# Last layer of a four-layer network: TensorE takes the attention sums two groups back and between a group's two pairs of turned scores

## The chip, the cores and the metric

The kernel runs on one core of one Trainium2 chip. The metric is the device time of one execution in microseconds (us). The time before is 2976.93 us, the median of three runs that lay between 2975.23 and 2987.77.

## The reference

The network has four layers over x, float32 of shape (4, 1024, 128). Each layer normalizes x without weights and adds an attention-like block and a feed-forward block. Only the last layer matters here:

```python
qkv = (x @ W_qkv + b_qkv).reshape(b, s, h, 3 * hd)        # h = 16 heads of hd = 8
logits = jnp.einsum('bshd,bkhd->bhsk', q, k) / np.sqrt(hd)
logits = jnp.where(k_pos > q_pos, -jnp.inf, logits)       # s = 1024
attn = jax.nn.softmax(logits, axis=-1)
out = jnp.einsum('bhsk,bkhd->bshd', attn, v).reshape(b, s, d)
attention = out @ W_out + b_out
# experts: the two best of 8 for each token, C = 128, H = 512
h = new_gelu(x_flat @ w1[e].T + b1[e]); out_e = h @ w2[e].T + b2[e]
output = output + cw[:, e:e + 1] * out_e
```

## The kernel before

The stage in question is `attn3_stage`. It computes the last layer's attention and its experts together, as one sequence of **slots** written out by hand. An item is one batch with one set of four heads; there are 16 items (4 batches, 4 sets). In slot s TensorE does three things with three different items.

- **Plain scores** of item s (`score`, L2138): queries on the partitions, keys along the row. VectorE takes the largest of each row from them (`largest`, L2354). There are 20 such units in an item; `SHARE` spreads them over the slot as 2, 2, 1, 1, 2, 2, 2, 2, 2, 2, 1, 1. A unit on the diagonal adds its mask by four more short matmuls (L2154). Here the units are called S.
- At the slot's start it turns the maxima of item s - 1 (`turn_max`, L2159), once VectorE has reduced the last unit of the slot before and put the maxima together (L2452). GpSimd splits them into bfloat16 parts, and they go by DMA into extra rows beside the queries.
- **Turned scores** of item s - 2 (`scoreT`, L2164): keys on the partitions, queries along the row, the maxima subtracted by the extra rows. ScalarE takes the exponential (`exps`, L2301). GpSimd zeroes the triangle of a diagonal tile (`causal`, L2487). Then TensorE multiplies by the values (`sums`, L2181), four float32 matmuls, one for each head, side by side in one bank.

A slot has 12 **groups**, one for each pair of a 512-query half and a 128-key tile: groups 0 to 3 belong to the first half, 4 to 11 to the second. Groups 0 to 3 and 8 to 11 lie on the diagonal and are 512, 384, 256 and 128 queries wide; the others are 512 wide. A group wider than 256 has four turned units and is issued as two pairs, here T0 and T2; a narrower one has two units and one pair, T0 alone. The order in a group is T0, S, T2, S, then the sums of the group before, then extras.

The **extras** are: XT (turn the rows of an expert tile, L2203, groups 0 to 3), UP (first expert matmul, L2211, a burst at group 4; ScalarE's gelu, L2321, follows each), DOWN (second expert matmul, L2222, from group 7), X (turn the finished sums, `turn_sums` L2196; half 1 of the item before in group 2, half 0 in group 6), A and Y (turn the merged heads and project them out, L2232 and L2244, in every fourth slot, groups 4 and 5, then 8 and 9). There are 39 expert tiles over slots 2 to 13, three or four in a slot. In slots 14 to 17 GpSimd gathers the experts' outputs, two indirect DMAs behind each of its triangles (L2491, L2496). Slots 16 and 17 have no S.

Three resources set when TensorE may go on.

- The **score ring**: two pairs of PSUM banks. S, the turned maxima, XT, DOWN, X, A and Y all take the next pair in turn, and each waits until the one two places before it has been read by VectorE:

```python
def take_s(*key):
    n = s_at[key]
    if n >= 2:
        pe.wait_ge(s_read, n - 1)
    return sbank(n)
```

- The **turned ring**: three banks for T and UP. A pair waits until the unit two before its first has been read by ScalarE (L2171). T2 thus waits for the first exponential of T0, and the next T0 for the first exponential of T2.
- One bank for the sums. ScalarE copies it out after each half (`out`, L2294: half 1 after the exponentials of the next item's group 0, half 0 after those of group 4, ahead of the gelus), and the first sums of the next half wait for that copy (L2185).

Of the kernel before, what the change touches and what calls it, by code (L numbers as in the profile page):

```python
# [1674 lines left out]
NI = B * NG  # L1675
# [224 lines left out]
GROUPS = len(TILES)  # L1900
SHARE = (2, 2, 1, 1, 2, 2, 2, 2, 2, 2, 1, 1)
BURST = 4
FIRST_SLOT, LAST_SLOT = 2, 13
PER_SLOT = {s: range((s - FIRST_SLOT) * NTILE // (LAST_SLOT + 1 - FIRST_SLOT),
                     (s + 1 - FIRST_SLOT) * NTILE // (LAST_SLOT + 1 - FIRST_SLOT))
# [22 lines left out]
TU = [list(turned_units(g)) for g in range(GROUPS)]  # L1928
# [7 lines left out]
def merged_batch(s):  # L1936


    return (s - 6) // 4 if s >= 6 and (s - 6) % 4 == 0 else None


def ring_tables():

    s_at, t_at = {}, {}

    def add(table, key):  # L1950
        table[key] = len(table)

    for s in range(SLOTS + 1):
        b = s - 2
        back = 0 <= b < NI
        if 0 <= s - 1 < NI:
            add(s_at, ("Z", s - 1))
        for g in range(GROUPS):
            if back:
                for i in range(len(TU[g])):  # L1960
                    add(t_at, ("E", b, g, i))
            for i in range(sum(SHARE[:g]), sum(SHARE[:g + 1])) if s < NI else ():
                add(s_at, ("S", s, i))
            for j, kt in enumerate(tiles_of(s)):
                if g == j:
                    add(s_at, ("XT", kt))
                if g == BURST:
                    for x in range(2):
                        add(t_at, ("UP", kt, x))
                if g == 7 + j:  # L1970
                    add(s_at, ("DOWN", kt))
            if g == 2 and b >= 1:
                add(s_at, ("X", b - 1, 1))
            if g == 6 and back:
                add(s_at, ("X", b, 0))
            if merged_batch(s) is not None and g in (4, 5):
                add(s_at, ("A", merged_batch(s), g - 4))
            if merged_batch(s) is not None and g in (8, 9):
                add(s_at, ("Y", merged_batch(s), g - 8))
    return s_at, t_at  # L1980


def attn3_stage(k, R):
# [15 lines left out]
    with ExitStack() as ctx:  # L1999
# [19 lines left out]
        s_at, t_at = ring_tables()  # L2019
# [25 lines left out]
        with nc.Block() as block:  # L2045
# [81 lines left out]
            def _(pe):  # L2127
# [128 lines left out]
                for s in range(SLOTS + 1):  # L2256
                    f, b = s, s - 2
                    front, back = f < NI, 0 <= b < NI
                    bb = merged_batch(s)
                    if 0 <= s - 1 < NI:  # L2260
                        turn_max(s - 1)
                    for g in range(GROUPS):
                        units = range(sum(SHARE[:g]), sum(SHARE[:g + 1])) if front else ()
                        for i in range(0, len(TU[g]), 2):
                            if back:
                                scoreT(b, g, i)
                            if front and i // 2 < len(units):
                                score(f, units[i // 2])
                        for i in units[len(TU[g]) // 2:]:
                            score(f, i)  # L2270
                        if back and g > 0:
                            sums(b, g - 1)
                        if g == 0 and 0 <= b - 1:
                            sums(b - 1, GROUPS - 1)
                        for j, kt in enumerate(tiles_of(s)):
                            if g == j:
                                turn_rows(kt)
                            if g == BURST:
                                for x in range(2):
                                    up(kt, x)  # L2280
                            if g == 7 + j:
                                down(kt)
                        if g == 2 and 0 <= b - 1:
                            turn_sums(b - 1, 1)
                        if g == 6 and back:
                            turn_sums(b, 0)
                        if bb is not None and g in (4, 5):
                            turn_out(bb, g - 4)
                        if bb is not None and g in (8, 9):
                            out_project(bb, g - 8)  # L2290

            @block.scalar
            def _(act):
                def out(c, half):  # L2294

                    act.wait_ge(sums_done, c * GROUPS + (4, GROUPS)[half])
                    if c > 0:
                        act.wait_ge(s_done, s_at["X", c - 1, half] + 1)
                    act.copy(oT[:, half, :], k.ps[:, bankO, :]).then_inc(sums_copied, 1)  # L2299

                def exps(c, g):  # L2301
                    w = WIDTH[g]
                    for i, (r, es) in enumerate(TU[g]):
                        n = t_at["E", c, g, i]
                        act.wait_ge(t_done, n + 1)
                        if i == 0 and c * GROUPS + g >= 3:
                            act.wait_ge(sums_done, c * GROUPS + g - 2)
                        hd = 2 * r + es[0]
                        dst = pT[:, g % 3, hd:hd + len(es), 0:w]
                        src = k.ps[:, tbank(n), 0:len(es) * w].rearrange("p (h q) -> p h q", q=w)  # L2310
                        act.activation(dst, src, ACT.Exp).then_inc(t_read, 1)  # L2311

                def gelu(kt, x):

                    n = t_at["UP", kt, x]
                    act.wait_ge(t_done, n + 1)
                    if kt >= 4:
                        act.wait_ge(s_done, s_at["DOWN", kt - 4] + 1)
                    for f in range(HALF_F):
                        ff = x * HALF_F + f  # L2320
                        a = act.activation(h[:, kt % 4, ff, :], k.ps[:, tbank(n), f * NSLOT:(f + 1) * NSLOT],  # L2321
                                           ACT.Gelu_apprx_tanh, bias=b1[:, kt % 4, ff:ff + 1])
                    a.then_inc(t_read, 1)

                for s in range(2, SLOTS + 1):
                    c = s - 2
                    for g in range(GROUPS):
                        if c < NI:
                            exps(c, g)
                        if g == 0 and c > 0:  # L2330
                            out(c - 1, 1)
                        if g == 4 and c < NI:
                            out(c, 0)
                        if g == BURST:
                            for kt in tiles_of(s):
                                act.wait_ge(s_t[kt % 4], 16 * 4 * (kt // 4 + 1))
                                for x in range(2):
                                    gelu(kt, x)

            @block.vector  # L2340
            def _(dve):
# [85 lines left out]
                for s in range(SLOTS + 1):  # L2427
                    f, b = s, s - 2
                    bb = merged_batch(s)
                    if 0 <= s - 1 < NI:  # L2430
                        turned_max(s - 1)
                    for g in range(GROUPS):
                        for i in range(sum(SHARE[:g]), sum(SHARE[:g + 1])) if f < NI else ():
                            largest(f, i)
                        for j, kt in enumerate(tiles_of(s)):
                            if g == j:
                                rows_turned(kt)
                            if g == 7 + j:
                                down_done(kt)
                        if g == 2 and 0 <= b - 1:  # L2440
                            norm(b - 1, 1)
                        if g == 6 and 0 <= b < NI:
                            norm(b, 0)
                        if bb is not None and g in (4, 5):
                            out_turned(bb, g - 4)
                        if bb is not None and g in (8, 9):
                            residual(bb, g - 8)
                    if f < NI:
                        dve.wait_ge(s_read, s_at["S", f, len(SU) - 1] + 1)
                        if f >= 2:  # L2450
                            dve.wait_ge(s_done, s_at["Z", f - 2] + 1)
                        dve.tensor_reduce(m[:, f % 2, :], mx[:, f % 2].rearrange("p r e t x -> p (r e t) x"), AX_X, ALU.max)\  # L2452
                           .then_inc(max_done, 1)
                    if s - 1 in GATHER:
                        combine(GATHER[s - 1])
# [215 lines left out]
```

## Time and profile before

| | |
|---|---|
| median of 3 runs | 2976.93 us (2975.23 to 2987.77) |
| profiled execution | 2986.29 us, span 2984.6 us |
| TensorE busy | 2085.2 us, 70% of the span |
| VectorE, ScalarE, GpSimd busy | 64%, 48%, 45% |
| this stage, slots 2 to 17 | from about 2236 to 2956 us of the span |

A timeline row has a start, a length, engine, line, operation, output and inputs, the partitions and elements, and how many instructions the row joins. In brackets stands the recorded idle time before it and the instruction that ended it. Matmuls are pipelined: a row's length includes the way through the array, so the time that a step takes of TensorE is read from start to start. A float32 matmul shows as two records. The line numbers are those of the kernel before; in the changed kernel every line behind the new constant stands one or a few lower.

### The profile page before, as it was taken

Reading aid. Unit: us, or ns where it says so; the run is one execution under the profiler, and the core shown is the slowest. Engines: PE = TensorE matmul, PEld = TensorE weight load, DVE = VectorE, ACT = ScalarE, POOL = GpSimd, SP = SyncE. Lnnn points to the kernel's source line nnn. Section 1 sums busy time; section 2 is a strip of 40 time slices with the busy share of each in tenths; the row PEclk is TensorE's granted clock in tenths of the full one; section 3 lists DMA queues with packets and bytes.
Section 4 is the critical chain, followed back from the end, with each engine's and each line's share of the span. In section 5 each row is a group of like instructions: output and inputs, shape, how many; then the busy total and the mean of one; then the engine's idle time right before and its main releaser. Section 6 shows DMA issues by size and latency. Waiting matters only on the chain. (4 is left out here: it accounts for less than half of the span.)

```text
span 2984.6 us, 35273 instructions
## 1 busy us (share of the span) xinstructions
PE 2085.2 (70%) x10366; PEld 1067.6 (36%) x10366; DVE 1922.1 (64%) x2484; ACT 1445.0 (48%) x2523; POOL 1328.7 (45%) x974
## 2 busy tenths in 40 slices
PE   2677786868777666856562688865048888888875
PEld 1233232323323223424341466653014444444422
DVE  6379888888988896683336677773155555656551
ACT  1476665666666652713341433332206656655553
POOL 2277777777777784022002566633521101111253
PEclk9899998989889898878766798876559999999875
DMA  1333434444444442001200000002321322313111
GB/s 39 88 129 126 133 125 128 134 127 136 127 123 133 122 142 73 0 1 50 84 20 0 1 0 0 0 0 50 98 81 46 87 75 65 90 51 87 28 29 49
DMA packets 146984, 214.72 MB, mean 72 GB/s; under 512 B 30746, under 2 KB 58292, under 8 KB 146228
## 3 DMA queue, kind: packets, MB, share of 16 engines
q1 hardware_dynamic: 142756, 204.72, 22.7%
q0 software_dynamic: 4096, 8.40, 1.3%
q8 instruction: 64, 1.05, 0.1%
q14 instruction: 68, 0.56, 0.1%
HBM read 193.91 MB, written 23.86 MB: 73 GB/s over the span
## 5 line engine op out<-in xcount | busy, mean ns | idle before, releaser
L505 PE MATMUL ps<-m_hC,ident 128*128 128x512 f32 x1024 | 547.4, 669 | 241.4 <-DVE m_hC L777 129.5
L694 POOL TENSOR_TENSOR m_dBx<-m_du,m_rowB 128x1024 f32<-128x1024 f32 x256 | 602.7, 2385 | 20.9 <-DVE m_h L768 20.9
L2311 ACT ACTIVATE a_pT<-ps 128x512 f32<-128x512 f32 (+2 forms) x640 | 319.7, 553 | 392.8 <-PE ps L2176 390.9
L2361 DVE TENSOR_REDUCE a_mx<-ps 128x2 f32<-128x1024 f32 (+2 forms) x320 | 349.1, 1116 | 165.1 <-PE ps L2154 126.3
L623 ACT ACTIVATE ps<-m_delta,m_A 128x512 f32<-128x512 f32 x512 | 341.6, 685 | 159.4 <-DVE m_h L768 158.4
L505 PEld LDWEIGHTS ps<-m_hC,ident 128*128 128x128 f32 x1024 | 198.8, 207 | 561.1 <-DVE m_hC L777 213.8
L768 DVE TENSOR_TENSOR_SCAN m_h<-ps,m_carry,m_dBx 128x512 f32<-128x512 f32 x256 | 311.4, 1265 | 74.4 <-ACT ps L623 53.7
L768 DVE TENSOR_TENSOR_SCAN m_h<-ps,m_dBx 128x512 f32<-128x512 f32 x256 | 295.9, 1206 | 63.2 <-ACT ps L623 34.8
L2491 POOL TENSOR_SCALAR_AFFINE_SELECT a_pT<-a_pT 128x512 f32<-128x512 f32 x128 | 81.6, 637 | 517.0 <-ACT a_pT L2311 516.4
L704 POOL TENSOR_TENSOR m_hC<-m_h,m_rowC 128x1024 f32<-128x1024 f32 x64 | 155.9, 2436 | 226.2 <-DVE m_h L768 226.2
L777 DVE TENSOR_TENSOR m_hC<-m_h,ps 128x1024 f32<-128x1024 f32 x192 | 234.2, 1220 | 15.2 <-issue 1.3
L2149 PE MATMUL ps<-a_k,a_q 48*128 48x512 bf16 (+3 forms) x768 | 139.4, 365 | 110.1 <-DMA a_k<-qk_parts 93.8
L633 ACT COPY ps<-m_rowC 128x512 f32<-128x512 f32 x192 | 112.1, 584 | 187.0 <-DVE m_hC L777 186.3
L2191 PE MATMUL ps<-a_pT,l_v 128*9 128x512 f32 (+3 forms) x1536 | 185.9, 560 | 21.7 <-POOL a_pT L2491 21.4
L2176 PE MATMUL ps<-a_q,a_k 51*128 51x512 bf16 (+3 forms) x768 | 129.9, 363 | 70.0 <-ACT a_pT L2311 68.5
L1611 PE MATMUL ps<-c_triu_adt,ones 128*128 128x512 f32 x64 | 53.6, 933 | 93.5 <-ACT c_triu_adt L1582 93.5
L460 PE MATMUL ps<-pad,m_wk 128*128 128x512 f32 x256 | 117.5, 604 | 1.1 <-DVE m_diag L726 1.1
L2176 PEld LDWEIGHTS ps<-a_q,a_k 51*128 51x128 bf16 x768 | 32.5, 95 | 190.6 <-ACT a_pT L2311 156.3
L266 PE MATMUL ps<-ident,n_xn 128*128 128x128 f32 x128 | 35.4, 431 | 84.9 <-DVE n_xn L246 84.8
L1889 POOL DMA_INDIRECT expert_rows<-l_xn,l_slot x64 | 65.3, 1020 | 63.1 <-DVE p_cmp L1855 43.9
L2149 PEld LDWEIGHTS ps<-a_k,a_q 48*128 48x128 bf16 x768 | 40.0, 99 | 129.9 <-issue 94.3
L2228 PEld LDWEIGHTS ps<-a_w,a_h 128*128 128x128 f32 x624 | 73.8, 194 | 34.4 <-DVE a_mx L2361 22.2
(361 smaller groups left out, 3872.2 us busy)
## 6 DMA issues: line engine op xcount, KB each, us to landing
m_rowB<-bc_rows SPq DMA_DIRECT2D x256, 256.0 KB, 3.8
m_rowC<-bc_rows SPq DMA_DIRECT2D x256, 256.0 KB, 3.7
a_w<-in_L3f_w1T SPq DMA_DIRECT2D x39, 256.0 KB, 2.5
a_w<-in_L3f_w2T SPq DMA_DIRECT2D x39, 256.0 KB, 3.2
qk_parts<-p_part SPq DMA_DIRECT2D x24, 256.0 KB
expert_rows<-in_zero_rows SPq DMA_DIRECT2D x39, 128.0 KB, 2.6
a_xs<-expert_rows SPq DMA_DIRECT2D x39, 128.0 KB, 2.2
expert_out<-a_y SPq DMA_DIRECT2D x39, 128.0 KB, 3.1
```

Of the source, the lines that this page charges most:

```text
L460: mm = pe.matmul(o, wk[:, d, tap, c * P:c * P + P], pad[:, b * ROW + shift:b * ROW + shift + CH], start=tap == 0, stop=tap == CONV - 1)
L505: mm = pe.matmul(ps[:, bankY + c, :], k.ident[:], hC[:, n % 3, c, :], start=False, stop=n % NS == NS - 1)
L623: act.activation(ps[:, bankA + m % 3, :], delta[:, i % 2, c, chunk(i, x)], ACT.Exp, scale=An[:, ITEMS[i][0], c, s:s + 1]).then_inc(decayed, 1)
L694: pool.tensor_tensor(dBx[:, n % 3], du[:, i % 2, :, chunk(i, x)], rowB[:, n % 4, :].unsqueeze(1).to_broadcast([P, HALF, CH]), ALU.mult).th ...
L704: pool.tensor_tensor(hC[:, n % 3], h[:, n % 3], rowC[:, n % 4, :].unsqueeze(1).to_broadcast([P, HALF, CH]), ALU.mult).then_inc(hc_pool, 1)
L768: dve.tensor_tensor_scan(time(h[:, n % 3, c, :]), time(ps[:, bankA + m % 3, :]), time(dBx[:, n % 3, c, :]), first, ALU.mult, ALU.add).then ...
L777: dve.tensor_tensor(hC[:, n % 3], h[:, n % 3], ps[:, bankC, :].unsqueeze(1).to_broadcast([P, HALF, CH]), ALU.mult).then_inc(hc_dve, 1)
L2149: mm = pe.matmul(k.ps[:, bank + r, j * w:j * w + w], qs[u][rows, e, t * P:t * P + P], ks[u][rows, e, x:x + w], start=True, stop=not diag, ...
L2176: mm = pe.matmul(k.ps[:, tbank(n + r), j * w:j * w + w], ks[u][rows, e, kt * P:kt * P + P], qs[u][rows, e, q0:q0 + w], start=True, stop=Tr ...
L2191: mm = pe.matmul(k.ps[32 * hd:32 * hd + HD + 1, bankO, CH - w:CH], R["v"][:, c, kt, hd, :], pT[:, g % 3, hd, 0:w], start=kt == 0, stop=kt ...
L2311: act.activation(dst, src, ACT.Exp).then_inc(t_read, 1)
L2361: dve.tensor_reduce(mx[:, c % 2, :, es[0]:es[0] + len(es), t, x // CH], src, AX_X, ALU.max)\
```

## The change

It adds a lag of two groups for the sums and puts them between T0 and T2. Both S units of a four-unit group then follow T2 back to back (`SHARE` has no 3, so the branch that would put one ahead of T2 is never taken). X moves from groups 2 and 6 to 4 and 8, A from 4 and 5 to 6 and 7, Y from 8 and 9 to 9 and 10. ScalarE copies the sums out one group later, which for half 0 is behind the gelus and no longer ahead of them.

```diff
+LAG = 2
...
                     for g in range(GROUPS):
-                        units = range(sum(SHARE[:g]), sum(SHARE[:g + 1])) if front else ()
-                        for i in range(0, len(TU[g]), 2):
-                            if back:
-                                scoreT(b, g, i)
-                            if front and i // 2 < len(units):
-                                score(f, units[i // 2])
-                        for i in units[len(TU[g]) // 2:]:
+                        units = list(range(sum(SHARE[:g]), sum(SHARE[:g + 1]))) if front else []
+                        if back:
+                            scoreT(b, g, 0)
+                        if back and g >= LAG:
+                            sums(b, g - LAG)
+                        if g < LAG and 0 <= b - 1:
+                            sums(b - 1, GROUPS - LAG + g)
+                        if back and len(TU[g]) > 2:
+                            if len(units) > 2:
+                                score(f, units.pop(0))
+                            scoreT(b, g, 2)
+                        for i in units:
                             score(f, i)
-                        if back and g > 0:
-                            sums(b, g - 1)
-                        if g == 0 and 0 <= b - 1:
-                            sums(b - 1, GROUPS - 1)
...
-                        if g == 2 and 0 <= b - 1:
+                        if g == 4 and 0 <= b - 1:
                             turn_sums(b - 1, 1)
-                        if g == 6 and back:
+                        if g == 8 and back:
                             turn_sums(b, 0)
-                        if bb is not None and g in (4, 5):
-                            turn_out(bb, g - 4)
-                        if bb is not None and g in (8, 9):
-                            out_project(bb, g - 8)
+                        if bb is not None and g in (6, 7):
+                            turn_out(bb, g - 6)
+                        if bb is not None and g in (9, 10):
+                            out_project(bb, g - 9)
...
                             exps(c, g)
-                        if g == 0 and c > 0:
+                        if g == LAG - 1 and c > 0:
                             out(c - 1, 1)
-                        if g == 4 and c < NI:
+                        if g == LAG + 3 and c < NI:
                             out(c, 0)
```

VectorE's order and the ring's table follow the same moves.

The first place is TensorE in group 7 of a slot with expert tiles. L2176 is T, L2149 S, L2191 the sums, L2228 DOWN. Before, the group and the T0 of the next:

```order
 L2176 MATMUL ps<-a_q,a_k 128x512 x2
 L2149 MATMUL ps<-a_k,a_q 128x512 x2
 L2176 MATMUL ps<-a_q,a_k 128x512 x2
 L2149 MATMUL ps<-a_k,a_q 128x512 x2
 L2191 MATMUL ps<-a_pT,l_v 9x512 x4
 L2228 MATMUL ps<-a_w,a_h 128x128 x8
 L2176 MATMUL ps<-a_q,a_k 128x512 x2
```

and now (lines one lower):

```order
 L2177 MATMUL ps<-a_q,a_k 128x512 x2
 L2192 MATMUL ps<-a_pT,l_v 9x512 x4
 L2177 MATMUL ps<-a_q,a_k 128x512 x2
 L2150 MATMUL ps<-a_k,a_q 128x512 x4
 L2229 MATMUL ps<-a_w,a_h 128x128 x8
 L2177 MATMUL ps<-a_q,a_k 128x512 x2
```

The sums have gone in front of T2, and DOWN now stands directly behind two S units.

The second place is TensorE in groups 10 and 11, at the end of a slot; L2154 is the mask of an S unit and L2162 turns the maxima. Before:

```order
 L2176 MATMUL ps<-a_q,a_k 128x256 x4
 L2149 MATMUL ps<-a_k,a_q 128x512 x2
 L2154 MATMUL ps<-a_consts_bf 128x128 x4
 L2191 MATMUL ps<-a_pT,l_v 9x384 x4
 L2176 MATMUL ps<-a_q,a_k 128x128 x4
 L2149 MATMUL ps<-a_k,a_q 128x512 x2
 L2154 MATMUL ps<-a_consts_bf 128x128 x4
 L2191 MATMUL ps<-a_pT,l_v 9x256 x4
 L2162 MATMUL ps<-ident,a_m 32x128
```

and now:

```order
 L2177 MATMUL ps<-a_q,a_k 128x256 x4
 L2192 MATMUL ps<-a_pT,l_v 9x512 x4
 L2150 MATMUL ps<-a_k,a_q 128x512 x2
 L2155 MATMUL ps<-a_consts_bf 128x128 x4
 L2177 MATMUL ps<-a_q,a_k 128x128 x4
 L2192 MATMUL ps<-a_pT,l_v 9x384 x4
 L2150 MATMUL ps<-a_k,a_q 128x512 x2
 L2155 MATMUL ps<-a_consts_bf 128x128 x4
 L2163 MATMUL ps<-ident,a_m 32x128
```

No sums stand any more between the slot's last S unit and the turning of the maxima.

The third place is ScalarE from group 4 on, in a slot with three tiles (L2311 exponentials, L2299 the copy of the sums, L2321 gelus). Before:

```order
 L2311 ACTIVATE a_pT<-ps 128x512 x4
 L2299 COPY a_oT<-ps 128x512
 L2321 ACT_TABLE_LOAD
 L2321 ACTIVATE a_h<-ps,a_b 128x256 x12
 L2311 ACT_TABLE_LOAD
 L2311 ACTIVATE a_pT<-ps 128x512 x16
```

and now:

```order
 L2313 ACTIVATE a_pT<-ps 128x512 x4
 L2323 ACT_TABLE_LOAD
 L2323 ACTIVATE a_h<-ps,a_b 128x256 x12
 L2313 ACT_TABLE_LOAD
 L2313 ACTIVATE a_pT<-ps 128x512 x4
 L2301 COPY a_oT<-ps 128x512
 L2313 ACTIVATE a_pT<-ps 128x512 x12
```

The copy has moved from ahead of the gelus to behind the exponentials of group 5.

## Rows read from the trace of the kernel before

**Rows 1.** Busy time by stretch (length, then engines in us, count; PEclk), the stage
```profile
2240.00:2860.00 620.00, 532.08 (x4704) 269.44 (x4703) 355.10 (x443) 370.52 (x743) 112.89 (x197) 0.94 0.23 65
2860.00:2984.60 124.60, 80.81 (x491) 23.82 (x487) 37.23 (x95) 52.17 (x105) 52.55 (x65) 0.64 0.14 39
```

**Rows 2.** The same view, slots 7 and 12, three tiles each
```profile
2473.46:2516.04 42.58, 35.83 (x343) 18.48 (x344) 25.76 (x32) 28.00 (x56) 6.76 (x13) 1.00 0.24 64
...
2703.61:2748.95 45.34, 38.79 (x344) 19.12 (x344) 25.76 (x32) 28.01 (x56) 6.75 (x13) 0.92 0.25 72
```

**Rows 3.** Waits, 2260 to 2860 us: total, times, longest
```profile
ACT a_pT L2311 <- PE ps L2176: 240.7, 143, 7.6
...
PE ps L2176 <- ACT a_pT L2311: 52.9, 92, 2.0
```

**Rows 4.** Timeline of TensorE, group 7 of slot 8 (start, length)
```profile
2542.57 0.39 PE L2176 MATMUL ps<-a_q,a_k 51*128 51x512 bf16 x2
2542.80 0.38 PE L2149 MATMUL ps<-a_k,a_q 48*128 48x512 bf16 x2
2543.64 0.39 PE L2176 MATMUL ps<-a_q,a_k 51*128 51x512 bf16 x2 [0.47 <-ACT a_pT L2311]
2543.87 0.38 PE L2149 MATMUL ps<-a_k,a_q 48*128 48x512 bf16 x2
2544.18 1.05 PE L2191 MATMUL ps<-a_pT,l_v 128*9 128x512 f32 x8
2545.16 2.05 PE L2228 MATMUL ps<-a_w,a_h 128*128 128x128 f32 x16
```

**Rows 5.** Timeline of ScalarE and VectorE in the same group
```profile
2542.99 2.16 ACT L2311 ACTIVATE a_pT<-ps 128x512 f32<-128x512 f32 x4 [1.27 <-PE ps L2176]
...
2543.22 2.36 DVE L2361 TENSOR_REDUCE a_mx<-ps 128x2 f32<-128x1024 f32 x2
```

**Rows 6.** Timeline of TensorE, the end of slot 8
```profile
2557.68 0.38 PE L2149 MATMUL ps<-a_k,a_q 48*128 48x512 bf16 x2
...
2558.40 0.62 PE L2191 MATMUL ps<-a_pT,l_v 128*9 128x256 f32 x8 [0.23 <-POOL a_pT L2491]
2559.84 0.27 PE L2162 MATMUL ps<-ident,a_m 128*32 128x128 f32 x1 [0.82 <-DVE a_m L2452]
```

**Rows 7.** Timeline of ScalarE and TensorE around the burst, slot 8
```profile
2527.86 0.59 ACT L2299 COPY a_oT<-ps 128x512 f32<-128x512 f32 x1
...
2529.84 4.63 ACT L2321 ACTIVATE a_h<-ps,a_b 128x256 f32<-128x256 f32 x12
...
2536.43 0.39 PE L2176 MATMUL ps<-a_q,a_k 51*128 51x512 bf16 x2 [1.99 <-ACT a_pT L2311]
...
2536.97 1.81 PE L2191 MATMUL ps<-a_pT,l_v 128*9 128x512 f32 x8
```

**Rows 8.** Timeline of TensorE and VectorE, groups 0 and 1 of slot 8
```profile
2516.47 0.22 PE L2149 MATMUL ps<-a_k,a_q 48*128 48x128 bf16 x2
...
2517.55 0.28 PE L2149 MATMUL ps<-a_k,a_q 48*128 48x256 bf16 x2
...
2518.09 0.41 PE L2191 MATMUL ps<-a_pT,l_v 128*9 128x128 f32 x8
...
2519.49 0.34 PE L2149 MATMUL ps<-a_k,a_q 48*128 48x384 bf16 x2 [0.35 <-DVE a_mx L2361]
...
2517.09 0.69 DVE L2361 TENSOR_REDUCE a_mx<-ps 128x4 f32<-128x512 f32 x1 [0.46 <-PE ps L2154]
2518.20 1.23 DVE L2361 TENSOR_REDUCE a_mx<-ps 128x4 f32<-128x1024 f32 x1 [0.42 <-PE ps L2154]
```

**Rows 9.** Timeline of GpSimd and TensorE, slots 15 and 16
```profile
2868.65 0.64 POOL L2491 TENSOR_SCALAR_AFFINE_SELECT a_pT<-a_pT 128x512 f32<-128x512 f32 x1 [9.48 <-ACT a_pT L2311]
...
2875.36 1.04 PE L2191 MATMUL ps<-a_pT,l_v 128*9 128x256 f32 x8 [1.63 <-POOL a_pT L2491]
...
2892.03 0.64 POOL L2491 TENSOR_SCALAR_AFFINE_SELECT a_pT<-a_pT 128x512 f32<-128x512 f32 x1
```

More of the change, by code:

```diff
@@ L1971, in ring_tables @@
                     add(s_at, ("DOWN", kt))
-            if g == 2 and b >= 1:
+            if g == 4 and b >= 1:
                 add(s_at, ("X", b - 1, 1))
-            if g == 6 and back:
+            if g == 8 and back:
                 add(s_at, ("X", b, 0))
[L1976 to L1979, printed above, removed]
+            if merged_batch(s) is not None and g in (6, 7):
+                add(s_at, ("A", merged_batch(s), g - 6))
+            if merged_batch(s) is not None and g in (9, 10):
+                add(s_at, ("Y", merged_batch(s), g - 9))
     return s_at, t_at
@@ L2282, in _ @@
                                 down(kt)
-                        if g == 2 and 0 <= b - 1:
+                        if g == 4 and 0 <= b - 1:
                             turn_sums(b - 1, 1)
-                        if g == 6 and back:
+                        if g == 8 and back:
                             turn_sums(b, 0)
-                        if bb is not None and g in (4, 5):
-                            turn_out(bb, g - 4)
-                        if bb is not None and g in (8, 9):
-                            out_project(bb, g - 8)
+                        if bb is not None and g in (6, 7):
+                            turn_out(bb, g - 6)
+                        if bb is not None and g in (9, 10):
+                            out_project(bb, g - 9)
             @block.scalar
@@ L2439, in _ @@
                                 down_done(kt)
-                        if g == 2 and 0 <= b - 1:
+                        if g == 4 and 0 <= b - 1:
                             norm(b - 1, 1)
-                        if g == 6 and 0 <= b < NI:
+                        if g == 8 and 0 <= b < NI:
                             norm(b, 0)
[L2444 to L2447, printed above, removed]
+                        if bb is not None and g in (6, 7):
+                            out_turned(bb, g - 6)
+                        if bb is not None and g in (9, 10):
+                            residual(bb, g - 9)
                     if f < NI:
```

## The prediction

> **What bounds the kernel now.** I read the busy time by stretch first, then the waits, then single groups on the timelines. Only the last layer's attention stage changes. In its long part TensorE is busy 532 of 620 us at a clock of 0.94 of full; its rest has a clock of 0.64 [rows 1]. A slot with three expert tiles that kept the full clock took 42.58 us with TensorE busy 35.83 [rows 2], so 6.75 us of the slot are recorded idle. Read from start to start, where the way through the array isn't counted as work, the waits come to about 8 us a slot. TensorE sets the pace by its work plus its waits, and ScalarE mostly waits for it: 240.7 us against 52.9 the other way [rows 3]. The reader is to see that the wait which the change attacks is real. In group 7 T0 starts at 2542.57 and T2 at 2543.64, 1.07 later, with 0.23 for T0 and 0.31 for one S unit between (2542.57 to 2542.80; 2543.87 to 2544.18) [rows 4]; 0.53 is left idle. That time is the exponential's: ScalarE starts 0.42 after T0 and takes 0.54 for one of its four [rows 5].
>
> **What the change removes.** TensorE's instructions stay the same, so a slot changes by its waits alone. The sums of a 512-wide group take 0.98 (2544.18 to 2545.16) [rows 4]. T0 and sums make 1.21, more than 1.07, so T2 no longer waits where such sums stand before it. Six groups of a slot (0, 4, 6, 7, 8, 9) wait so now, about 0.5 each: 3.0. Narrow sums remain in front of T2 in groups 0, 1 and 4 (256, 128 and 256 wide; scaled from 0.98 to about 0.5, 0.25 and 0.5), and these still wait about 1.1 together. Also removed are the waits for GpSimd's triangle (0.23 to 0.29 in group 11 [rows 6]) and VectorE waits of 0.8 in groups 1 and 2 (one is 0.35 [rows 8]). The copy of half 0 leaves the way of the gelus, 0.59 [rows 7], and X of half 1 moves into the time in which TensorE waits for the burst (the 1.99 behind the gelus [rows 7]); burst waits fall from 3.3 to 2.5. Removed: 3.0 - 1.1 + 0.3 + 0.8 + 0.8 = 3.8 us a slot.
>
> **What it adds.** (a) *The score ring.* VectorE needs 2.36 for two 1024-wide units [rows 5], and TensorE may be two ring places ahead and no more. Before, the two S units of a group stood 1.07 apart with the sums behind them, and what came next found the older unit read. Now S, S and the extra come within 0.6 us, and the extra waits for the first S of its own group. A unit's read starts 0.42 after an unmasked S (as ScalarE's after T0) and 0.62 after a masked one (2516.47 to 2517.09); TensorE goes on 0.06 after the read's end (2518.20 + 1.23 to 2519.49) [rows 8]. Count from T2. Group 9: S at 0.17, read from 0.59 to 1.80, DOWN at 1.86, TensorE free at 0.79: 1.07 of wait. Group 8 (768-wide unit, about 0.95): 0.8. Group 7: group 6 left two units, read until 3.1 after its T2; the next T2 comes 1.07 + 1.21 = 2.28 after it, so the first S of group 7 is read from 3.1 to 4.3, its second S waits 0.3 and DOWN 0.9. Group 0: S at 0.23, read from 0.85 to 1.54, XT at 1.60; the masked units take 0.37 and 0.54 (2517.55 to 2518.09 [rows 8]), TensorE is free at 1.14: 0.46. Group 1 likewise 0.8 behind VectorE's backlog, group 3 0.2. Sum 4.5. (b) *The slot's end.* From the last S to the turned maxima 2.16 pass (2557.68 to 2559.84 [rows 6]): VectorE's last read and the joining of the maxima. Before, sums lay in it, now nothing does; the recorded 0.82, 0.9 from start to start, becomes 2.16 - 0.43 = 1.75: 0.85 more. (c) *The copy.* Sums 4 stand behind T0 of group 6 and need the copy, which ScalarE makes behind the exponentials of group 5. From T2 of group 5 these end at 0.42 + 2 x 0.54, with one more in front, at 1.5; the copy ends at 2.15; T0 is out at 1.3: 0.85 of wait, and 0.2 before T0. The twin in group 2 is covered by XT's wait. Sum 1.05.
>
> Added: 4.5 + 0.85 + 1.05 = 6.4, net **+2.6 us in each of 12 tile slots**, +31. Slots 6 and 10 turn out a batch: A was partly in the burst's wait and now stands visible behind S, S: +1.6 each, +3; slot 14 the same without tiles, +1. Slots 15 to 17 gain. There GpSimd sets the pace: 2868.65 to 2892.03 for eight triangles with two gathers behind each, and TensorE waits up to 1.63 for one [rows 9]. From the last of these to the next slot's first, T2 of group 5 is no longer queued behind a fresh T0 (1.3) and X is out of the way (0.6, at the half clock 1.1), against the copy's 0.85: about -2, -1.5, -1.5, together -5. At an equal clock the sum is +30.
>
> **Clock.** TensorE falls to the lower level (1.2 GHz) in most slots, usually behind the burst: sums take 1.81 behind the 1.99 wait [rows 7] where they take 1.05 at 2.4 GHz [rows 4]. Slot 12 with 0.92 of the clock took 45.34, slot 7 with all of it 42.58 [rows 2]: such a stretch costs up to 2.8. Waits per slot rise from about 8.3 to 10.9, and the 1.75 at the slot's end stands close to those of group 0. I take two or three such stretches more than now, +6 in all, between none and one in each tile slot, 12 x 2.8 = 34. Sum: +36, of 2986.3 for the profiled execution 3022. That execution lay 9.4 above the median, so I forecast 2976.93 + 36 = **3013**.
>
> **Rivals.** *Clock* (slower still): every tile slot gets a second low stretch, 30 + 34 = +64: 3041. The waits at the slot's end speak for it; against it, slot 7 had 6.75 us of idle time and never fell. The Trainium skill (TensorE: Matmul & The Clock Gate, "A second HAM failure mode: psum-queue depth-cycling") tells of a kernel in which small idle stretches between PSUM banks make the clock swing to and fro. By that rule this rival would be the case; the trace before shows falls, but mostly behind long waits.
>
> *The ring doesn't bite* (faster): if VectorE has read the first S by the time TensorE reaches DOWN or XT, the 4.5 is gone, and of the rest +2.6 - 4.5 = -1.9 a slot remains, -23; with the tail's -5 and the +2 that is left of A's 4 it is -26: 2951. The place is DOWN in groups 7 to 9; it decides from a read that ends within 0.8 of T2, against 1.8 worked out above. For it speaks only that VectorE is idle 40% of the stage (355 of 620 busy [rows 1]); against it that the ring is two deep and the third item always needs the first.
>
> *No difference*: ring waits half as long, because an earlier wait in the same group moves T2 later and with it VectorE's backlog shrinks: 36 - 27 = +9, 2986.
>
> That the order isn't what the change says can be excluded: the rows of the order show the sums in front of T2 and both S units behind it.
>
> **Numbers.** A difference of 0.5% (14.9 us) is about what a measurement of this kernel can tell from none. Chances: forecast (2992 to 3030) 0.55, clock 0.15, no difference 0.16, ring doesn't bite 0.14. So slower 0.70, same 0.16, faster 0.14. The range leaves out most of the faster case and the far end of the clock's: 2965 to 3042.
>
> **What would show it.** TensorE's wait before T2 (52.9 now) should fall to under a half outside the burst; new waits of TensorE for VectorE's reads in front of DOWN of about 0.8 to 1.1 and of XT of 0.5 to 0.8; 1.7 instead of 0.82 before the turned maxima; about 0.85 for the copy before sums 4; three-tile slots at full clock of about 45 us; slots 15 to 17 shorter. If DOWN starts without a wait behind S, S, or if a full-clock slot is under 42.6, the prediction is wrong. A GpSimd wait in the tail that doesn't shrink would make only the -5 wrong.

## The result and the profile after

Before took 2984.34 us (median of six runs, 2975.23 to 2995.36), the changed kernel 3036.45 (six runs, 3028.38 to 3042.59). The ratio is **1.0174** with a 95% interval of 1.0145 to 1.0204: slower by 1.7%, or 52.1 us, where 36 us or 1.2% were forecast. The forecast of 3013 was worked out from a median before of 2976.93, of three runs; with six it is 7.4 higher. The profiled execution of the change took 3028.38 us, the lowest of its six.

First the busy time by stretch of the changed kernel. Columns: stretch, length, then busy us (count) of PE, PEld, DVE, ACT, POOL, the granted clock, DMA share, GB/s. The first three stretches are slots 2 to 13, 14 and 15, and 16 to the end; then slot 8 (three tiles, full clock), slot 6 (three tiles and a batch turned out) and slot 7 (three tiles, lower clock).

```profile
2231.96:2838.95 606.99, 499.50 (x4270) 258.27 (x4271) 316.13 (x400) 340.77 (x683) 80.95 (x156) 0.92 0.22 63
2838.95:2916.44 77.49, 63.35 (x578) 24.66 (x579) 50.23 (x59) 41.60 (x84) 40.06 (x54) 0.87 0.13 34
2916.44:3026.70 110.26, 69.53 (x373) 20.23 (x373) 24.58 (x81) 42.12 (x85) 49.59 (x58) 0.58 0.16 41
2532.34:2577.56 45.22, 36.03 (x344) 18.78 (x344) 25.48 (x32) 28.01 (x56) 6.75 (x13) 1.00 0.26 73
2425.97:2481.55 55.58, 45.91 (x392) 25.58 (x392) 29.50 (x38) 28.03 (x56) 6.74 (x13) 0.96 0.27 74
...
2481.55:2532.34 50.79, 42.59 (x344) 20.31 (x344) 25.59 (x32) 28.03 (x56) 6.75 (x13) 0.84 0.20 58
```

The same stretches of before:

```profile
2236.19:2798.22 562.03, 485.56 (x4279) 251.34 (x4279) 318.69 (x400) 340.92 (x683) 81.09 (x156) 0.94 0.24 68
2798.22:2876.33 78.11, 62.69 (x578) 23.66 (x579) 51.79 (x63) 41.74 (x84) 40.37 (x54) 0.88 0.13 35
2876.33:2984.60 108.27, 68.40 (x369) 20.24 (x365) 23.53 (x77) 42.20 (x85) 45.99 (x58) 0.59 0.15 42
```

The tile slots lose 45.0 us, slots 14 and 15 gain 0.6, the rest loses 2.0; what comes before the stage ran 4.2 shorter in this execution, though nothing in it changed, so the two spans differ by 42.1. A three-tile slot at full clock takes 45.22 where it took 42.58 [rows 2]: +2.64 with nearly the same work (36.03 against 35.83). The four-tile slots at full clock take 49.50 against 46.66 (+2.84), slot 6 takes 55.58 at 0.96 against 51.92 at 0.97 for slot 10 before (+3.66). Waits alone thus make 7 x 2.64 + 3 x 2.84 + 2 x 3.66 = 34.3, and the clock makes up the remaining 10 or so. Slot 7 shows it: 50.79 at 0.84 for the work that took 45.22.

TensorE's longest waits after the change, from 2260 to 2860 us (total, times, longest). L2229 is DOWN, L2177 T (T0 and T2 alike), L2163 the turned maxima, L2209 XT, L2192 the sums:

```profile
ACT a_pT L2313 <- PE ps L2177: 258.8, 177, 6.4
...
PE ps L2229 <- DVE a_mx L2363: 34.3, 36, 1.1
...
PE ps L2177 <- ACT a_pT L2313: 21.5, 20, 1.7
PE ps L2163 <- DVE a_m L2454: 20.0, 12, 1.7
...
PE ps L2209 <- DVE a_mx L2363: 9.4, 15, 0.8
...
PE ps L2192 <- ACT a_oT L2301: 7.0, 13, 0.6
```

The wait before T2, 52.9 us in 92 places [rows 3], is down to 21.5 in 20. The eleven longest of these, 1.7 each, stand behind the burst and make 19.2; outside it 2.3 are left, where before had 32.3. In place of these waits stand 34.3 before DOWN and 9.4 before XT, both for VectorE's reads, and 20.0 at the slots' ends. The timeline of TensorE in slot 8, groups 7 to 9 and the end (start, length):

```profile
2557.01 0.39 PE L2177 MATMUL ps<-a_q,a_k 51*128 51x512 bf16 x2
2557.33 1.04 PE L2192 MATMUL ps<-a_pT,l_v 128*9 128x512 f32 x8
2558.31 0.39 PE L2177 MATMUL ps<-a_q,a_k 51*128 51x512 bf16 x2
2558.54 0.85 PE L2150 MATMUL ps<-a_k,a_q 48*128 48x512 bf16 x4
2560.24 2.05 PE L2229 MATMUL ps<-a_w,a_h 128*128 128x128 f32 x16 [0.85 <-DVE a_mx L2363]
...
2565.25 2.05 PE L2229 MATMUL ps<-a_w,a_h 128*128 128x128 f32 x16 [0.78 <-DVE a_mx L2363]
...
2570.79 2.05 PE L2229 MATMUL ps<-a_w,a_h 128*128 128x128 f32 x16 [1.11 <-DVE a_mx L2363]
...
2577.56 0.27 PE L2163 MATMUL ps<-ident,a_m 128*32 128x128 f32 x1 [1.67 <-DVE a_m L2454]
```

The sums fill the time between T0 and T2 and T2 comes without a wait, as meant. Then S, S and DOWN follow at once, and DOWN waits 0.85, 0.78 and 1.11 for the read of the first S of its own group. In group 7 the two S units take 0.85 where such a pair takes 0.60 in group 9, so the second S waits 0.25 too.

### The profile page after: what moved, and what is told of

The parts are those of the page before. It is cut to its first block and busy times, and to the rows that moved or that the text cites. A ratio compares the mean times of both kernels' runs of the same rounds, so it can differ in the third digit from the quotient of the medians.

```text
span 3026.7 us, 35273 instructions
## 1 busy us (share of the span) xinstructions
PE 2095.5 (69%) x10366; PEld 1070.3 (35%) x10366; DVE 1918.7 (63%) x2484; ACT 1444.6 (48%) x2523; POOL 1332.6 (44%) x974
## 5 line engine op out<-in xcount | busy, mean ns | idle before, releaser
L2192 PE MATMUL ps<-a_pT,l_v 128*9 128x512 f32 (+3 forms) x1536 | 189.1, 570 | 25.8 <-POOL a_pT L2493 17.2
L2177 PE MATMUL ps<-a_q,a_k 51*128 51x512 bf16 (+3 forms) x768 | 134.3, 375 | 37.8 <-ACT a_pT L2313 32.5
L2229 PE MATMUL ps<-a_w,a_h 128*128 128x128 f32 x624 | 80.0, 281 | 34.3 <-DVE a_mx L2363 34.3
L2177 PEld LDWEIGHTS ps<-a_q,a_k 51*128 51x128 bf16 x768 | 33.5, 96 | 178.0 <-ACT a_pT L2313 149.3
```

The costliest lines, as they stand in the source:

```text
L2177: mm = pe.matmul(k.ps[:, tbank(n + r), j * w:j * w + w], ks[u][rows, e, kt * P:kt * P + P], qs[u][rows, e, q0:q0 + w], start=True, stop=Tr ...
L2192: mm = pe.matmul(k.ps[32 * hd:32 * hd + HD + 1, bankO, CH - w:CH], R["v"][:, c, kt, hd, :], pT[:, g % 3, hd, 0:w], start=kt == 0, stop=kt ...
```

## The experiments

Four explanations stood against each other for the extra time: the **score ring** (DOWN and XT behind S, S), the **slot's end** (nothing between the last S and the turned maxima), the **clock** that falls through the longer waits, and the moved X, A and Y or the copies. Each run has its own comparison with before on its own chip, where before took 2988.8 to 2999.7 us, so runs are compared by their ratios. In all diffs a line of "..." stands for what is left out.

### The moves alone, and the sums alone

Before, with X, A and Y in their new groups and nothing else (TensorE shown; VectorE and the ring's table follow):

```diff
-                        if g == 2 and 0 <= b - 1:
+                        if g == 4 and 0 <= b - 1:
                             turn_sums(b - 1, 1)
-                        if g == 6 and back:
+                        if g == 8 and back:
...
-                        if bb is not None and g in (4, 5):
-                            turn_out(bb, g - 4)
-                        if bb is not None and g in (8, 9):
-                            out_project(bb, g - 8)
+                        if bb is not None and g in (6, 7):
+                            turn_out(bb, g - 6)
+                        if bb is not None and g in (9, 10):
+                            out_project(bb, g - 9)
```

> The kernel before with X, A and Y alone moved as the change moves them (X to groups 4 and 8, A to 6 and 7, Y to 9 and 10); sums and score units stand as before. Theory R (score ring: the cost of the change comes from two score units back to back in front of an extra): no S, S, extra here, so no cost from it; X of half 1 hides in the burst's wait (-0.6 in each of 12 tile slots, -7), A comes out of it in slots 6 and 10 (+1 each), and in slots 16 and 17 the late X lets VectorE's sums over the gathered rows fall on GpSimd's triangle of group 9 (+1.6 each). Together about -5 to +3 us, ratio 0.998 to 1.001. Rival M (the moves of the extras cost the 52 us): ratio 1.010 or more. In the trace TensorE's waits in front of DOWN for VectorE stay near zero.

Measured: 0.9973 (0.9949 to 0.9998), a little under the 0.998 to 1.001 expected. A three-tile slot at full clock, by stretch:

```profile
2509.14:2550.87 41.73, 35.55 (x344) 18.63 (x344) 25.73 (x32) 27.99 (x56) 6.75 (x13) 1.00 0.27 78
```

That is 0.85 less than 42.58: X of half 1 now lies in the wait behind the burst. The moves gain and are not the cost. The other half is the changed kernel with those moves undone (X in groups 2 and 6, A in 4 and 5, Y in 8 and 9):

> The changed kernel with X, A and Y back in their old groups; sums two groups back between the pairs, S units back to back. Theory R: DOWN and XT still wait 0.5 to 1.1 each, ratio 1.013 to 1.020, like the change; X in group 6 stands behind S, S and waits too (+0.8 a slot) but no longer in group 8, and the triangle of group 9 in slots 16 and 17 is back at 0.64. Rival M: falls back to 1.000 to 1.005.

Measured: 1.0279 (1.0244 to 1.0314), more than expected. TensorE's waits, 2230 to 2830 us, L2201 being X:

```profile
PE ps L2229 <- DVE a_mx L2363: 30.1, 32, 1.1
...
PE ps L2201 <- DVE a_mx L2363: 16.0, 21, 1.0
```

The waits before DOWN are there without any move, and X, standing behind S, S in groups 2 and 6, gets one too. The moves are worth about 1% to the changed kernel. Its tile slots ran at clocks of 0.80 to 0.96; how much of the excess that makes was not separated.

### The ring: one S ahead of the sums

The changed kernel, with the first S of each group ahead of the sums, so that the two S units stand apart again:

```diff
                         if back:
                             scoreT(b, g, 0)
+                        if units:
+                            score(f, units.pop(0))
                         if back and g >= LAG:
                             sums(b, g - LAG)
```

> The changed kernel with the first S unit of each group ahead of the sums: T0, S, sums two back, T2, S, extra. T2 waits for nothing and the first S of a group is read by the time the extra comes; at the slot's end sums lie again between the last S and the turned maxima. Theory R: all ring waits (4.5 a slot) and the slot's end (0.85) go, T0 to T2 takes 1.5 instead of 1.2; a three-tile slot at full clock takes 39.5 to 41 us (42.6 before, 45.2 changed): ratio 0.985 to 0.992 against the kernel before. Rival L (late sums themselves, with the copy of the sums behind group 5 and group 1, are the cost): stays at 1.005 or above.

Measured: **0.9865** (0.9827 to 0.9903), as expected, and faster than both kernels. By stretch (the same kind of slot), and TensorE's waits from 2230 to 2830 us:

```profile
2282.15:2322.68 40.53, 35.54 (x344) 18.57 (x344) 25.89 (x32) 27.94 (x56) 6.75 (x13) 1.00 0.27 79
```

```profile
PE ps L2163 <- DVE a_m L2456: 13.0, 14, 1.8
...
PE ps L2229 <- DVE a_mx L2365: 3.1, 8, 0.5
```

The wait before DOWN falls from 34 us to 3 and the slot from 45.22 to 40.53. All waits of TensorE for the ring (DOWN, XT, X, A and S) fall from 47.0 to 15.7, of which S itself now has 10.1. The wait at the slot's end falls with them, to 0.9 in most slots, so this run alone doesn't separate the two; the next one does. The idea of the change holds; what cost the time is that it left the two S units side by side.

### The ring: the extra between the two S units

The changed kernel with XT and DOWN after the first S of the group (so also in the ring's table and on VectorE):

```diff
-                        for i in units:
+                        for i in units[:1]:
                             score(f, i)
                         for j, kt in enumerate(tiles_of(s)):
                             if g == j:
                                 turn_rows(kt)
+                            if g == 7 + j:
+                                down(kt)
+                        for i in units[1:]:
+                            score(f, i)
+                        for j, kt in enumerate(tiles_of(s)):
...
-                            if g == 7 + j:
-                                down(kt)
```

> The changed kernel with XT and DOWN between the two S units of a group, everything else as changed: T0, sums, T2, S, DOWN, S. The extra now needs the S of the group before, long read. Theory R: DOWN and XT start without a wait, a three-tile slot at full clock takes about 41 us with the wait at the slot's end still 1.67: ratio 0.990 to 1.000. Rival L, and rival C (the clock alone): DOWN's waits go but the ratio stays above 1.010.

Measured: 1.0119 (1.0080 to 1.0158); a time at or under before's was expected, and that missed: 1.0119 lies where the clock alone was said to put it (above 1.010). By stretch, and the waits from 2230 to 2830 us (L2166 is the turned maxima here):

```profile
2331.37:2373.98 42.61, 36.08 (x343) 18.71 (x344) 25.64 (x32) 28.01 (x56) 6.75 (x13) 1.00 0.25 73
```

```profile
PE ps L2166 <- DVE a_m L2463: 20.1, 12, 1.8
```

At full clock the slot is as short as before's (42.61 against 42.58), and no wait before DOWN is left; S itself waits 13.2 in 30 places. In the profile the tile slots lose 28 us against before, and seven of them, which ran at 0.79 to 0.89 of the clock, lose 30. The wait at the slot's end was left as in the change, so the next four runs took that up.

### The slot's end

The change with the last group's S alone ahead of the sums:

```diff
+                        if g == GROUPS - 1 and units:
+                            score(f, units.pop(0))
                         if back and g >= LAG:
```

> The changed kernel with one S unit moved: in group 11 the last S goes ahead of the sums, so that sums lie again between it and the turned maxima. The wait there should be 0.8 to 0.9 instead of 1.67, a three-tile slot at full clock 44.4 us instead of 45.2. Theory W (waits alone): 14 slots x 0.85 = -12 us, ratio 1.013 where the change has 1.017. Theory C (the 1.67 wait also makes the clock fall at the start of slots, where the changed kernel has 8 stretches at 1.2 GHz and the kernel before two): those stretches go too, and the ratio is 1.006 to 1.010.

Measured: 1.0128 (1.0110 to 1.0146), the time expected if the waits alone count. But the waits were not as expected. VectorE and TensorE at the end of slot 12, with three tiles:

```profile
2781.38 2.36 DVE L2365 TENSOR_REDUCE a_mx<-ps 128x2 f32<-128x1024 f32 x2 [1.32 <-PE ps L2155]
2783.77 0.22 DVE L2456 TENSOR_REDUCE a_m<-a_mx 128x32 f32<-128x64 f32 x1
...
2784.14 0.27 PE L2163 MATMUL ps<-ident,a_m 128*32 128x128 f32 x1 [1.59 <-DVE a_m L2456]
```

Behind such slots the wait hardly moved: the S units of groups 10 and 11 are still read back to back (2.36 for both) and VectorE ends no earlier. It is VectorE's backlog of two units, not the last S alone. Behind the six slots in which DOWN or Y stands between these two units (5, 6, 9, 10, 13 and 14) the same edit did bring the wait to 0.27 to 0.95. The tile slots took 599.2 in sum, 7.8 less than in the change, but slots 14 and 15 ran at 0.74 of the clock and took 93.7 instead of 77.5; why is open. Both edits together:

> The changed kernel with XT and DOWN between the two S units of a group and, in group 11, the last S ahead of the sums. With the first alone a three-tile slot at full clock took 42.6 us, as much as before the change (42.6), and yet the ratio was 1.012. Theory C (the rest was the clock's, from falls behind the wait at the slot's end): full-clock slot 41.8, falls at the slots' starts gone, ratio 0.990 to 0.996. Theory W: 1.012 less 12 us, 1.008.

Measured: 1.0040 (1.0020 to 1.0059), between the two times expected (0.990 to 0.996, and 1.008); seven slots still begin with 1.59. With both S units of groups 10 and 11 ahead of the sums (`g >= GROUPS - 2` in the edit above):

> The changed kernel with the last two S units of a slot (groups 10 and 11) ahead of the sums of their groups. With group 11 alone the wait at the slot's end stayed at 1.59 and a full-clock slot at 45.0 us, because VectorE still had both last units to read, 2.36 us, after the second came. Theory V (VectorE's backlog sets the slot's end): now the unit of group 10 is read early, the wait is 0.8 to 0.9, a three-tile slot at full clock takes 44.2 to 44.5 and the ratio is 1.008 to 1.012. Rival (the wait there isn't VectorE's): 1.6 again and 45.0.

Measured: 1.0073 (1.0048 to 1.0098), a little under the 1.008 to 1.012 expected, with a wait of 0.27 to 0.94 before the turned maxima in slots 3 to 16. The tile slots took 587.83 in sum, 19.2 less than in the change, though slots of like clock (0.96) differ by only 0.4: 46.06 there, 45.62 to 45.71 here. Twelve times 0.4 is 5, so I estimate that some 14 of the 19 came from the clock. Then the reverse, in before: only the last S of a slot put behind the sums.

```diff
-                            if front and i // 2 < len(units):
+                            if front and i // 2 < len(units) and g < GROUPS - 1:
                                 score(f, units[i // 2])
...
                             sums(b, g - 1)
+                        if front and g == GROUPS - 1:
+                            score(f, units[0])
```

> The kernel before with one S unit moved: in group 11 the last S comes behind the sums instead of ahead of them, so the wait before the turned maxima is 1.67 instead of 0.82 and nothing else of the change is in it. Theory W: 14 slots x 0.85 = +12 us, ratio 1.004. Theory C: stretches at 1.2 GHz now begin right behind that wait in half of the slots, at 1.2 to 2.8 us each, ratio 1.007 to 1.012.

Measured: **1.0095** (1.0078 to 1.0112), as expected. TensorE at the start of a slot (start, length):

```profile
2525.94 0.37 PE L2162 MATMUL ps<-ident,a_m 128*32 128x128 f32 x1 [1.67 <-DVE a_m L2454]
2526.25 0.61 PE L2176 MATMUL ps<-a_q,a_k 51*128 51x512 bf16 x2
```

The wait is 1.67 instead of 0.82 [rows 6], and right behind it T takes 0.61 where it takes 0.39 in full-clock groups: the clock is at 1.2 GHz. Such a stretch begins within 2.5 us of the slot's start in 11 of the 13 slots 3 to 15 here, in two of before and in 8 of the change. In the run before this one, with its 0.9, it does so in two, both ahead of the start, and in the changed kernel with half reads (next section), where the wait is 1.13, in none. Of the 29.7 us lost, 14 x 0.85 = 12 are the wait itself. So one longer wait costs more through the clock than by its own length. The Trainium skill (TensorE: Matmul & The Clock Gate, "A second HAM failure mode: psum-queue depth-cycling") tells of a kernel that cycles through PSUM banks and in which frequent small idle stretches between groups of matmuls make the clock swing. The trace agrees that waits of this kind let it fall and come back, though here it is one wait in a slot of about 45 us, made longer by 0.85, that decides.

### VectorE's reading time

The change, and then before, with VectorE reading only the first half of the keys of each S unit, so that the maxima leave the other half out:

```diff
-                    src = k.ps[:, bank:bank + 2, 0:len(es) * w].rearrange("p r (e k) -> p r e k", k=w)
+                    src = k.ps[:, bank:bank + 2, 0:len(es) * w].rearrange("p r (e k) -> p r e k", k=w)[:, :, :, 0:w // 2]
```

> The changed kernel with VectorE reading only the first half of the keys of each S unit for the row maxima, so the maxima are over half the scores; all else is computed. A 1024-wide read of 1.22 us becomes one of 0.69. Theory R (the ring waits and the slot's end are VectorE's read time): the waits in front of DOWN fall from 0.8 to 1.1 down to 0.6 or less, and a full-clock slot from 45.2 to 41.5 to 42.0; ratio against the kernel before 0.994 to 1.000. Rival L (late sums or copies cost): the slot stays above 44.

> The kernel before with the same half reads, the control of the run before: the maxima are over half the scores of each S unit. Theory R: it has few waits for VectorE, so it gains less, about 1.3 us a slot (its two S and X waits, the slot's end): full-clock slot 41.3, ratio 0.992 to 0.996. The gap of changed to before at full clock, 2.64 us with whole reads, should be 0.2 to 0.7 with half reads.

Measured: 0.9973 (0.9954 to 0.9993), as expected, and 0.9886 (0.9861 to 0.9910), faster than the 0.992 to 0.996 expected, each against the whole kernel before. By stretch and by waits (2230 to 2830 us), the changed one first:

```profile
2652.68:2695.19 42.51, 35.82 (x344) 18.78 (x344) 16.03 (x32) 28.02 (x56) 6.75 (x13) 1.00 0.24 67
```

```profile
PE ps L2229 <- DVE a_mx L2363: 18.3, 36, 0.6
PE ps L2163 <- DVE a_m L2454: 13.6, 12, 1.1
```

```profile
2448.28:2489.95 41.67, 35.65 (x344) 18.57 (x344) 16.90 (x32) 28.00 (x56) 6.75 (x13) 1.00 0.22 61
```

The gap between change and before shrinks from 2.64 to 0.84 a slot (0.2 to 0.7 expected; the changed slot takes 42.51, for 41.5 to 42.0) and from 1.7% to 0.9%. That the price of the change goes with VectorE's reading time is shown; half-length reads still leave half of DOWN's wait.

### The copies, and the tail

Two variants of the run with S first. In one, ScalarE makes its copies between the two pairs of exponentials of groups 1 and 5:

```diff
                     for i, (r, es) in enumerate(TU[g]):
+                        if i == 2 and g == LAG - 1 and c > 0:
+                            out(c - 1, 1)
+                        if i == 2 and g == LAG + 3:
+                            out(c, 0)
...
```

> The kernel with the first S ahead of the sums (0.9865) and in it ScalarE's copies of the sums moved between the two pairs of exponentials of groups 1 and 5 instead of behind them. TensorE's wait for the copy before sums 0 and sums 4 (4.2 us in all, and hidden waits behind it) goes, but the second pair of exponentials comes 0.55 later and the next T0 with it. If the wait is what costs: -0.4 in each of 16 slots and twice, about -8 us, ratio 0.983 to 0.985. If the delay only changes place: 0.986 to 0.988.

Measured: 0.9862 (0.9843 to 0.9882), no different from 0.9865: TensorE's wait for the copy (4.2 in all) goes, its wait for the exponentials rises from 25.4 to 30.0, and the delay only changes place. The other puts X of half 0 back into group 6 in the slots without tiles:

```diff
-                        if g == 8 and back:
+                        if g == (6 if s > LAST_SLOT else 8) and back:
                             turn_sums(b, 0)
...
```

> The kernel with the first S ahead of the sums (0.9865), and X of half 0 back in group 6 in slots 14 to 17 alone. Theory P (VectorE's sums over the gathered rows, which follow X in its order, slow GpSimd's triangle of group 9): in slots 16 and 17 that triangle takes 0.64 instead of about 2 us, and the chain of eight triangles 21.1 us instead of about 22.7; -3 to -5 us, ratio 0.984 to 0.986. Rival (the long triangle has another cause): it stays at 2 us or more.

Measured: 0.9857 (0.9836 to 0.9879), median 2945.35 us, the lowest of all, though not to be told apart from 0.9865. The reason for trying it is in the tail of the changed kernel, on GpSimd and VectorE in slot 16 (the triangles of groups 8 and 9):

```profile
2947.53 0.64 POOL L2493 TENSOR_SCALAR_AFFINE_SELECT a_pT<-a_pT 128x512 f32<-128x512 f32 x1 [11.75 <-ACT a_pT L2313]
...
2950.52 2.29 POOL L2493 TENSOR_SCALAR_AFFINE_SELECT a_pT<-a_pT 128x512 f32<-128x512 f32 x1
```

```profile
2947.93 4.39 DVE L2424 SCALAR_TENSOR_TENSOR x_tm<-l_xn,l_cwr,x_tm 128x128 f32<-128x128 f32 x16
```

The second triangle takes 2.29 instead of 0.64 while VectorE adds up the experts' outputs from two inputs in SBUF, and ends 0.49 after the last of the sixteen additions (2950.52 + 2.29 = 2952.81, against 2947.93 + 4.39 = 2952.32). The same triangle in slot 17 takes 2.03. The Trainium skill (SBUF — State Buffer, "SBUF: two separate sides") says that such an operation and one of GpSimd that reads SBUF share a port pair, held by one at a time. The trace agrees, and in it additions that follow each other at once keep the triangle out to the last of them. It can also go the other way: where the two met at 2877.67 before, and at 2918.16 in the change, the triangle took its 0.64 or 0.65 and one addition 1.18 instead of 0.34. What decides between the two is open. Those additions follow X in VectorE's order, and the change moved X onto the triangles. The triangle of group 9 in slot 17 with S first, and with X back in group 6:

```profile
2908.07 1.85 POOL L2495 TENSOR_SCALAR_AFFINE_SELECT a_pT<-a_pT 128x512 f32<-128x512 f32 x1 [0.19 <-ACT a_pT L2315]
```

```profile
2903.09 0.65 POOL L2495 TENSOR_SCALAR_AFFINE_SELECT a_pT<-a_pT 128x512 f32<-128x512 f32 x1
```

## Why the prediction was right, and where it was off

The mechanism was forecast and the runs show it; the size was put too low. Of the range, 2965 to 3042, the measured 3036.45 lies 6 us under the upper end. It lies outside the 2992 to 3030 that the prediction gave to its own forecast, and it is nearer to the 3041 of the clock rival than to 3013 (with the base of six runs the two would be 3048 and 3020, and it is nearer to the rival still). That it lies in the range at all is owed in part to the range's width.

- **Removed waits**: right. T2 waits 2.3 instead of 32.3 outside the burst, where under a half was forecast, and X went into the burst's wait (0.85 a slot by itself, 0.8 forecast).
- **(a) The score ring**: right in place and size. DOWN waits 0.85, 0.78 and 1.11 in groups 7, 8 and 9, against 0.9, 0.8 and 1.07; XT waits 0.41 and 0.78 in groups 0 and 1, against 0.46 and 0.8. With the 0.25 of the second S it makes 4.2 in slot 8, for 4.5. Three runs show it from both sides: the waits stay without the moves, fall to a third when the S units stand apart, and DOWN's halve with the read. So the ring that "doesn't bite" is excluded.
- **(b) The slot's end**: right, 1.67 recorded. (The working's 2.16 - 0.43 is 1.73 and not 1.75, which changes nothing.) The last S by itself doesn't make it: after the change VectorE has the units of groups 10 and 11 before it, and where nothing stands between these only both moved together bring 0.9 back.
- **(c) The copy**: over-sized a little. Sums 4 wait 0.57 by the record, 0.73 from start to start, for 0.85.
- **Net per slot**: +2.64 at full clock for +2.6; slots with a batch +3.66 for +4.2. By waits the tile slots lose 34.3, as forecast (31 + 3).
- **Slots 15 to 17**: wrong. Forecast was -5; measured +0.4 (slot 15 -1.6, slots 16 and 17 +2.0), while slot 14 lost 0.9 for 1. The rows that the prediction took for the way "to the next slot's first" triangle lead from the triangle of group 3 to that of group 8 in the same slot. In slot 17 that way did fall by 1.4, from 15.5 (2928.77 to 2944.25) to 14.1 (2970.86 to 2984.97), in slot 16 by only 0.3. Against it stand the two slowed triangles: the eight from group 8 of slot 16 to group 3 of slot 17 took 22.68 from first start to last instead of 21.07, the last four 10.57 instead of 9.13. The step counted X's own time and not what VectorE does behind X.
- **Clock**: right in kind, under-sized: +6 forecast, about 10 in the profile. "Two or three such stretches more" were five in the tile slots, 15 instead of 10. Counted by slots' starts they are six more, and the run with the last S behind the sums shows that the wait there brings them on. The rival's second stretch in every tile slot did not come: slots 5, 8 and 13 kept the full clock.

Tail and clock, about 5 us each, make the step from the +36 forecast to the +46.3 of the stage (45.0 - 0.6 + 2.0). In the rest of the profile the change ran 4.2 shorter, and the profiled execution of before lay 2 above its median, that of the change 8 below: so the spans differ by 42 and the medians by 52. Open remain how the clock's share divides over single waits, and the full size of the run with the sums alone.

## What to carry to other kernels

In a ring two deep and worked in order, stand the units of a slow reader apart; whatever comes right behind two of them waits for the first. Keep some work between the last unit and the step that needs its result, and count the reader's whole backlog there. When a step moves, follow what stands behind it on the engines that read it.

## What was not expected of the hardware

- With a wait longer by 0.85 us at the slot's start, a stretch at 1.2 GHz began within 2.5 us of that start in 11 of 13 slots, and the kernel lost 29.7 us where the waits themselves make 12. Before, with 0.82 to 1.12 at the same place, it did so in two.
- GpSimd's triangle over 128x512 float32 took 1.85 to 2.29 us instead of 0.65 beside VectorE's additions from two SBUF inputs, 2.82 in the run with the moves alone. In all of these it ended 0.5 after the last of a row of additions that followed each other at once.
